# Router rows turned by DMA in an attention and mixture-of-experts kernel, with routing a half-step later

## The chip, the cores and the metric

The kernel runs on one core of a Trainium2 chip. The metric is the device time of one execution in microseconds, as the median over runs. The engines are named as in the profile: PE is TensorE (matmuls), with PEld its weight loads; DVE is VectorE, ACT is ScalarE, POOL is GpSimd, SP is SyncE, which issues most DMAs.

## What is computed

Gated cross-attention over a short context, then a mixture of experts, for 4 x 1024 tokens of width 256. Cut to what matters:

```python
x = x + tanh(g_xattn) * attn(layernorm(x), ctx, ctx, ...)     # 16 heads of 16, 77 keys, softmax(|q k| / 4)
n = layernorm(x)
logits = n @ w_router                                          # 256 x 8
probs = softmax(logits); topk_w, topk_idx = top_k(probs, 2)
h = gelu(n @ w1[e] + b1[e])                                    # 8 experts, 256 -> 1024 -> 256
out = sum over the two experts of topk_w[e] * (h @ w2[e] + b2[e])
x = x + tanh(g_ffn) * out
```

## The kernel before, in words

There are 32 tiles of 128 tokens; two tiles are a *pair*, 16 pairs in all. The attention phase goes through the pairs in half-steps: `even(j)` works on the scores of tile 2j, `odd(j)` on those of tile 2j + 1, and each half-step also carries a piece of work of older pairs. Every engine has its own `even` and `odd`, written out by hand, so the order on each engine is fixed in the program; semaphores (`ready`) order the engines against each other. The expert phase then takes tiles of 256 (later 128) routed rows.

What an older pair goes through in the kernel before, with j the pair of the half-step:

- `odd(j)`: the attention of pair j - 2 is projected into the bank PROJ (`project_attention`); VectorE adds it to x (`add_attention`, L1174) and takes the statistics of the sum (`row_statistics`).
- `even(j)`: GpSimd makes the factors (`norm_factors`), ScalarE the normalised rows of pair j - 3 (`normalise_row`) and their two-byte high half (`high_row`), which with the low half of `low_row` (VectorE, `odd(j)`) makes the row that is scattered to the experts.
- `odd(j)`: TensorE turns the normalised rows of pair j - 3 (`turn_rows`, four 128x128 transposes in four-byte values into the bank TURN), ScalarE copies them (`copy_rows`), TensorE multiplies them by the router's weights (`router_logits`, L1673) into the bank ROUTE, VectorE copies the logits out (`route(j, 1)`, L1142).
- `even(j)`: VectorE picks the two experts of pair j - 4 (`choose`), TensorE counts ranks (`ranks`, L1682 to L1686), VectorE makes the rows' places (`place_rows`) and the shares.
- `odd(j)`: GpSimd scatters the rows of pair j - 4 with four indirect DMAs (`scatter_rows`).

PROJ, TURN, NORM and ROUTE are the four banks that the scores use too. So TensorE waits ahead of each half-step's scores (`score_banks_free`) until what was left in them has been read; for the even half-step that is also `x2_sb`, the addition of the attention of the pair in the half-step before.

In the same half-steps the experts' weights are loaded and split: SyncE loads half a layer into `stage`, ScalarE makes the two-byte high half (`high_half`), VectorE the low half (`low_half`, L1128), and SyncE loads the next half once the low half is done. VectorE also splits the projected queries (`low_queries`, L1347) behind ScalarE's `high_queries`, and finds the largest score per head (`top_scores`, L1091).

After ten pairs have been routed (`EARLY_PAIRS`), VectorE plans the first six expert tiles (`plan_early`), so that the experts can begin before the last pairs are routed.

## Time and profile before

| | |
|---|---|
| Median of 3 runs | 660.27 us (655.99 to 662.45) |
| The profiled execution | 654.93 us, its span 653.1 us |
| Busy share of the span | PE 97%, PEld 86%, DVE 70%, ACT 51%, POOL 48% |
| Granted TensorE clock, mean | 0.989 |
| Attention phase, up to the first expert tile | some 258 us of the span |

The rows further down come from views of this one execution. The stretches give, between two times, how long each engine was busy, the granted TensorE clock (PEclk, 1.00 is full speed) and the share of the DMA engines. The timeline gives an engine's instructions in order of time, equal ones in a row merged; a bracket at a row's end is the idle time before it and what ended it. Matmul ends are modelled, so starts are what to compare on PE. The page's part on DMA issues and the view of one line give the time from a DMA's issue to its landing.

### The profile page before, as it was taken

The numbers are of one execution on the slowest core, as the hardware profiler recorded it, in microseconds if no ns is written. First come the engines' busy times: TensorE is split into PE (matmuls) and PEld (weight loads), VectorE is DVE, ScalarE is ACT, GpSimd is POOL, SyncE is SP. The second block draws the span as 40 slices with busy tenths as digits, with TensorE's granted clock in tenths as the row PEclk, the third lists the DMA queues.
The fourth block names the chain that finished last, engine by engine and source line by source line (L and its number), as shares of the span: only waits on it lengthen the run. The fifth ranks groups of instructions, "written<-read, shape, count | busy, mean of one in ns | idle before, by whom it ended". The sixth has DMA issues, their size and how long they took to land.

```text
span 653.1 us, 20940 instructions
## 1 busy us (share of the span) xinstructions
PE 633.6 (97%) x6637; PEld 562.7 (86%) x6638; DVE 459.7 (70%) x1298; ACT 333.8 (51%) x741; POOL 310.7 (48%) x420
## 2 busy tenths in 40 slices
PE   8999999999999999899999999999999999999993
PEld 7799999999999999798888888888888888888872
DVE  5687888888888896689665656556564647777773
ACT  4668777788778875623242323323242324444441
POOL 6423477777777455766352323334242433333333
PEclk9899999999999999899999999999999999999997
DMA  6144354555544445524954333333433344533322
GB/s 208 41 135 156 115 159 153 164 164 177 165 149 132 147 156 172 117 55 81 202 74 60 50 49 49 51 51 58 60 46 56 43 58 54 56 54 52 52 35 25
DMA packets 89157, 63.37 MB, mean 97 GB/s; under 512 B 51489, under 2 KB 84775, under 8 KB 88935
## 3 DMA queue, kind: packets, MB, share of 16 engines
q1 hardware_dynamic: 75519, 43.95, 26.0%
q0 software_dynamic: 13440, 18.14, 16.5%
q8 instruction: 58, 0.95, 0.6%
q14 instruction: 36, 0.29, 0.2%
q10 hardware_dynamic: 104, 0.04, 0.0%
HBM read 28.08 MB, written 24.63 MB: 81 GB/s over the span
## 4 chain that ended last, share of the span: by engine, by line
PE 57%; DMA 3%; DVE 2%; issue 1%; POOLq 0%; ACT 0%; SPq 0%; DVEq 0%; ACTq 0%
PE banks L1720 20%; PE banks L1703 20%; PE banks L1738 7%; PE banks L1752 7%; DMA out_dram<-prob_t,meta 2%; PE banks L1632 1%; DMA x_t<-routed 1%; PE banks L1659 1%; PE banks L1673 0%; PE banks L1613 0%; PE banks L1640 0%; DVE prob L1291 0%; POOLq L681 0%; DVE v_area L1293 0%; DVE top L1091 0%
## 5 line engine op out<-in xcount | busy, mean ns | idle before, releaser
L977 ACT ACTIVATE stage<-banks,bias_t 128x256 f32<-128x256 f32 x200 | 83.8, 470 | 169.6 <-PE banks L1703 157.1
L1703 PE MATMUL banks<-x_t,w_hi 128*128 128x256 f16 x800 | 133.9, 274 | 1.4 <-DMA x_t<-routed 1.4
L1720 PE MATMUL banks<-w,prob 128*128 x800 | 132.4, 273 | 0.6 <-DVE v_area L1293 0.6
L856 POOL DMA_INDIRECT out_dram<-prob_t,meta x46 | 74.7, 1625 | 99.7 <-DVE prob_t L1283 82.6
L1703 PE MATMUL banks<-x_t,w_lo 128*128 128x256 f16 x400 | 109.7, 274 | 0.0
L1720 PE MATMUL banks<-w,v_area 128*128 x400 | 109.1, 273 | 0.0
L1703 PEld LDWEIGHTS banks<-x_t,w_hi 128*128 x800 | 78.5, 98 | 11.1 <-issue 1.5
L986 ACT ACTIVATE stage<-banks,bias_t 128x128 f32<-128x128 f32 x168 | 52.6, 363 | 66.8 <-PE banks L1738 66.5
L1720 PEld LDWEIGHTS banks<-w,prob 128*128 128x128 f16 x800 | 78.1, 98 | 9.8 <-issue 0.8
L819 POOL DMA_INDIRECT routed<-row,pos x64 | 71.2, 1113 | 27.9 <-issue 14.6
L1632 PEld LDWEIGHTS banks<-v_area,prob_t 128*128 128x128 f32 x640 | 73.9, 192 | 4.3 <-DVE attn L1110 0.7
L1632 PE MATMUL banks<-v_area,prob_t 128*128 128x34 f32 (+1 forms) x640 | 77.2, 277 | 0.3 <-DVE attn L1110 0.3
L1738 PEld LDWEIGHTS banks<-x_t,w_hi 128*128 x672 | 58.1, 98 | 19.9
L1738 PE MATMUL banks<-x_t,w_hi 128*128 128x128 f16 x672 | 72.9, 219 | 0.0
L1263 DVE TENSOR_TENSOR v_area<-stage,prob 128x512 f16<-128x512 f32 x100 | 69.4, 694 | 3.4
L1279 DVE SCALAR_TENSOR_TENSOR prob_t<-banks,arena 128x256 f32<-128x256 f32 x50 | 21.0, 420 | 70.0 <-PE banks L1720 68.5
L842 POOL DMA_INDIRECT out_dram<-prob_t,meta x21 | 32.9, 1566 | 70.0 <-DVE prob_t L1311 57.4
L1738 PE MATMUL banks<-x_t,w_lo 128*128 128x128 f16 x336 | 64.3, 219 | 0.0
L1752 PE MATMUL banks<-w,prob 128*128 x168 | 62.9, 379 | 0.3 <-DVE v_area L1293 0.3
L1091 DVE TENSOR_REDUCE top<-prob 128x16 f32<-128x1232 f32 x32 | 45.8, 1431 | 21.2 <-ACT prob L896 21.2
L1261 DVE CAST prob<-stage 128x512 f16<-128x512 f32 x100 | 44.2, 442 | 15.4 <-ACT stage L977 13.5
L1613 PE MATMUL banks<-ident,prob 128*128 128x128 f32 x320 | 52.3, 279 | 0.1
(254 smaller groups left out, 1254.9 us busy)
## 6 DMA issues: line engine op xcount, KB each, us to landing
stage<-in_L_ffn_w_dram SPq DMA_DIRECT2D x32, 512.0 KB, 4.1
x_in<-in_x_dram SPq DMA_DIRECT2D x16, 256.0 KB, 3.6
x_res<-in_x_dram SPq DMA_DIRECT2D x16, 256.0 KB, 4.0
out_dram<-x_res SPq DMA_DIRECT2D x16, 256.0 KB, 2.9
routed<-turned SPq DMA_DIRECT2D x9, 265.0 KB, 4.8
out_dram<-prob_t,meta POOLq DMA_INDIRECT x67, 3.8
routed<-row,pos POOLq DMA_INDIRECT x64, 2.9
arena<-in_L_ffn_b_dram SPq DMA_DIRECT2D x1, 1024.0 KB, 7.8
```

Source lines behind the costliest of these rows:

```text
L819: pool.indirect_dma_start(routed[:, :], bass.IndirectOffsetOnAxis(ap=pos[:, held, tile, choice:choice + 1], axis=0), row[:, held, tile], N ...
L856: pool.indirect_dma_start(out[:, :], bass.IndirectOffsetOnAxis(ap=meta_of(j, pj)[:, b, E:E + 1].bitcast(U32), axis=0), y[:, pj, b], None, ...
L977: ins = act.activation(hid[:, c], H[:, q, c % PER * SLOTS:(c % PER + 1) * SLOTS], ACT.Gelu_apprx_tanh, bias=k.bias_t[:, bass.ds(e * HC + c ...
L986: ins = act.activation(small_part(hid_flat, q)[:, c * P:(c + 1) * P], H[:, q, c * P:(c + 1) * P], ACT.Gelu_apprx_tanh, bias=k.bias_t[:, ba ...
L1091: dve.tensor_reduce(top_part(i, 0), prob[:, i % 2, 0:SCORES].rearrange("p (h k) -> p h k", k=KEYS), AX.X, ALU.max).then_inc(top_sb, 1)
L1263: dve.tensor_tensor(h_lo[:, pj, part], hid[:, part], h_hi[:, pj, part], ALU.subtract)\
L1613: pe.matmul(T[:, g, c * P:(c + 1) * P], prob[:, i % 2, (first + c) * P:(first + c + 1) * P], k.ident[:], is_transpose=True, start=(c == 0) ...
L1632: mm = pe.matmul(V[:, first * VW:(first + n) * VW], prob_t[:, c, :], k.v_rows[:, b, c, 0:n * VW], start=(c == 0), stop=(c == PCH - 1), ski ...
L1703: mm = pe.matmul(H[:, q, c % PER * SLOTS:(c % PER + 1) * SLOTS], w[:, bass.ds(e, 1), i, c * P:(c + 1) * P].rearrange("p a n -> p (a n)"), ...
L1720: mm = pe.matmul(Y[pj][:, b * D:(b + 1) * D], h[:, pj, c, b * P:(b + 1) * P], w[:, bass.ds(e, 1), c, :].rearrange("p a n -> p (a n)"), sta ...
L1738: mm = pe.matmul(H[:, q, c % PER * P:(c % PER + 1) * P], w[:, bass.ds(e, 1), i, c * P:(c + 1) * P].rearrange("p a n -> p (a n)"), x[:, i], ...
L1752: mm = pe.matmul(Y[p][:, 0:width], h[p][:, c * P:(c + 1) * P], k.w2[:, bass.ds(e, 1), c].rearrange("p a i n -> p (a i n)")[:, 0:width], st ...
```

## The change

For pairs 0 to 11 (`TURNED_PAIRS = PAIRS - 4`) the rows are no longer turned by TensorE. SyncE turns the two-byte halves of the row, which lie in SBUF for the scatter anyway, with two transposing DMAs per pair (`turn_rows` on SyncE, in `odd(j)` for pair j - 3). TensorE multiplies them by two-byte halves of the router's weights, made once, 12 matmuls per pair (high by high, high by low, low by high, two chunks, two tiles), and does it a half-step later, in `even(j)` for pair j - 4. Everything behind it moves on by a half-step: `choose` to the end of VectorE's `even(j)`, `ranks` to `odd(j)`, `place_rows` and `shares` to VectorE's `odd(j)`, `scatter_rows` to the end of GpSimd's `even` of the next pair, `plan_early` to the start of VectorE's `even(15)`. The last four pairs keep the old way, and pair 12's copy of the turned rows comes behind both high halves on ScalarE. In VectorE's `odd(j)` the attention is added ahead of `low_half(j, 0)`, not behind it. The two-byte identity is read out of the four-byte one with a stride instead of being a copy. The diff, cut to its core:

```diff
@@ SyncE
+                    if 0 <= j - 3 < TURNED_PAIRS:
+                        turn_rows(j - 3)
+                def turn_rows(j):
+                    ready(sp, row_hi, j)
+                    ready(sp, row_lo, j)
+                    ready(sp, logit_ps, j - 1)
+                    for tile in range(2):
+                        sp.dma_start_transpose(rows_t[:, :, tile * P:(tile + 1) * P],
+                                               row[:, j % ROWS_HELD, tile, 0:D].bitcast(F16)).then_inc(rows_ld, 16)
@@ GpSimd, end of even(j); its odd(j) is empty now
+                    if exists(j - 5):
+                        scatter_rows(j - 5)
@@ ScalarE, odd(j)
                     if j > 0 and token_tile(i - 1):
                         copy_top(i - 1)
-                    if exists(j - 3):
-                        copy_rows(j - 3)
                     if exists(j):
                         high_half(j, 1)
+                    if j - 3 == TURNED_PAIRS:
+                        copy_rows(j - 3)
                     if exists(j + 2):
                         copy_normalised(j + 2)
+                    if exists(j - 4):
+                        route_exp(j - 4)
@@ VectorE, even(j)
+                    if j - 5 == EARLY_PAIRS:
+                        plan_early()
...
+                    if exists(j - 4):
+                        route(j - 4, 1)
...
                         normalise_attn(i - 2)
-                    if routed_pair:
-                        route(j - 4, 11, 1)
-                        route(j - 4, 12, 2)
+                    if exists(j - 4):
+                        choose(j - 4)
@@ VectorE, odd(j)
                         normalise_attn(i - 2)
+                    if exists(j - 4):
+                        if j - 4 == EARLY_PAIRS:
+                            ready(dve, rank_ps, j - 4)
+                            count_early()
+                        place_rows(j - 4)
+                    if exists(j - 2):
+                        add_attention(j - 2)
+                        row_statistics(j - 2)
+                    if j - 3 == TURNED_PAIRS:
+                        route(j - 3, 1)
+                    if exists(j - 4):
+                        shares(j - 4)
                     if exists(j):
                         low_half(j, 0)
-                    if exists(j - 2):
-                        add_attention(j - 2)
-                    if exists(j - 3):
-                        route(j - 3, 1)
-                    if exists(j - 2):
-                        row_statistics(j - 2)
@@ TensorE
                 def router_logits(j):
-                    ready(pe, x2t_sb, j)
                     ready(pe, places, j - 1, PLACE_OPS, 1)
+                    if j < TURNED_PAIRS:
+                        ready(pe, router_halves, 0, 2)
+                        ready(pe, rows_ld, j, 32)
+                        for tile in range(2):
+                            n = 0
+                            for c in range(KC):
+                                for x, w in ((c, router_hi), (c, router_lo), (KC + c, router_hi)):
+                                    mm = pe.matmul(ROUTE[:, tile * E:(tile + 1) * E], rows_t[:, x, tile * P:(tile + 1) * P],
+                                                   w[:, c], start=(n == 0), stop=(n == 3 * KC - 1))
...
@@ TensorE, even(j): -ranks(j - 4)  +router_logits(j - 4)
@@ TensorE, odd(j)
-                    if exists(j - 3):
+                    if exists(j - 4):
+                        ranks(j - 4)
+                    if j - 3 == TURNED_PAIRS:
                         turn_rows(j - 3)
```

What stands where on TensorE, in the odd half-step of the full swing, between the turned largest scores (`top`) and the probabilities. Before:

```order
L1600 MATMUL banks<-ident_bf,top 128x128
L1640 MATMUL banks<-ident,turned 128x128 x4
L1659 MATMUL banks<-x_t,turned 128x256 x4
L1673 MATMUL banks<-w_router,turned 128x8 x4
L1640 MATMUL banks<-ident,x_norm 128x128 x4
```

The turn of the rows, the attention's projection (L1659), the router product, the turn of the new pair's x. In the changed kernel, at the same place:

```order
L1619 MATMUL banks<-ident,top 128x128
L1713 MATMUL banks<-chosen,before 128x8
L1714 MATMUL banks<-seen,ones 128x8
L1715 MATMUL banks<-chosen,before 128x8
L1716 MATMUL banks<-seen,ones 128x8
L1717 MATMUL banks<-chosen,ones 128x8
L1678 MATMUL banks<-x_t,turned 128x256 x4
L1659 MATMUL banks<-ident,x_norm 128x128 x4
```

The four turns and the four-byte product are gone, the five rank matmuls have come in. In the even half-step the ranks stood ahead of the projection of the queries (L1809) before; in the changed kernel the 12 router matmuls stand there, of which the last two and what follows them are:

```order
L1696 MATMUL banks<-router_lo,rows_t 128x8
L1696 MATMUL banks<-router_hi,rows_t 128x8
L1840 MATMUL banks<-xn_t,x_t 128x256 x4
L1659 MATMUL banks<-ident,attn 128x128 x4
L1632 MATMUL banks<-ident,prob 128x128 x4
```

So the projection of the queries is behind more matmuls than it was. On VectorE, in the odd half-step from the attention of the tile (`attn`) on, before:

```order
L1110 TENSOR_TENSOR attn<-banks,den 128x256
L1128 SCALAR_TENSOR_TENSOR w_lo<-stage,w_hi 128x1024
L1174 SCALAR_TENSOR_TENSOR x_res<-banks,gates,x_res 128x512
L1142 COPY logits<-banks 128x16
L1117 BN_STATS stats<-x_res 128x6 x2
L1123 BN_AGGR mv<-stats 128x2 x2
L1145 MAX best<-logits 128x8 x2
```

In the changed kernel, at the same place:

```order
L1124 TENSOR_TENSOR attn<-banks,den 128x256
L1203 TENSOR_TENSOR place<-banks,region_of 128x16
L1206 TENSOR_TENSOR seen<-seen,chosen 128x8
L1208 TENSOR_TENSOR placed<-mask,place 128x32
L1212 TENSOR_REDUCE pos<-placed 128x4
L1213 TENSOR_TENSOR seen<-seen,chosen 128x8
L1189 SCALAR_TENSOR_TENSOR x_res<-banks,gates,x_res 128x512
L1131 BN_STATS stats<-x_res 128x6 x2
L1137 BN_AGGR mv<-stats 128x2 x2
L1177 TENSOR_REDUCE l_sum<-l_exp 128x2
L1179 RECIPROCAL l_rec<-l_sum 128x2
L1182 TENSOR_TENSOR share<-l_exp,l_rec 128x4
```

The low half of the weights (`w_lo`) stands behind the shares now; the five instructions of `place_rows` have come in ahead of the addition of the attention (`x_res`).

## Rows read from the trace of the kernel before

**Rows 1.** Stretches: length, busy time by engine, PEclk, DMA share, GB/s.

```profile
core 0: us, PE busy (x) PEld busy (x) DVE busy (x) ACT busy (x) POOL busy (x), PEclk, DMA share, GB/s
70.82:220.78 149.96, 149.96 (x1713) 140.11 (x1712) 128.25 (x426) 117.83 (x221) 108.81 (x170) 1.00 0.49 158
220.78:248.89 28.11, 27.48 (x330) 25.69 (x328) 25.04 (x89) 21.59 (x41) 15.03 (x23) 1.00 0.56 158
```

**Rows 2.** Timeline of TensorE over one pair: start, length, instruction.

```profile
130.80 0.58 PE L1572 MATMUL banks<-arena 32*128 32x154 f16 x24
...
133.62 0.17 PE L1682 MATMUL banks<-chosen,before 128*128 128x8 bf16 x1
...
133.75 1.97 PE L1809 MATMUL banks<-xn_t,x_t 128*128 128x256 f32 x8
...
137.76 0.58 PE L1572 MATMUL banks<-arena 32*128 32x154 f16 x24
...
140.58 0.61 PE L1640 MATMUL banks<-ident,turned 128*128 128x128 f32 x4
141.03 1.89 PE L1659 MATMUL banks<-x_t,turned 128*128 128x256 f32 x8
142.76 0.95 PE L1673 MATMUL banks<-w_router,turned 128*128 128x8 f32 x8
143.57 0.63 PE L1640 MATMUL banks<-ident,x_norm 128*128 128x128 f32 x4
144.04 0.60 PE L1613 MATMUL banks<-ident,prob 128*128 128x128 f32 x4
```

**Rows 3.** Timeline of VectorE over the same pair.

```profile
136.64 0.88 DVE L1347 SCALAR_TENSOR_TENSOR arena<-banks,bias_t,arena 128x256 f16<-128x256 f32 x2 [0.23 <-ACT arena L912]
...
138.05 0.15 DVE L1164 RECIPROCAL l_rec<-l_sum 128x2 f32<-128x2 f32 x1
...
138.32 0.75 DVE L1117 BATCH_NORM_STATS2 stats<-x_in 128x6 f32<-128x256 f32 x2
...
139.33 0.66 DVE L1269 TENSOR_TENSOR row<-turned,row 128x512 f16<-128x512 f32 x1
...
142.08 1.22 DVE L1128 SCALAR_TENSOR_TENSOR w_lo<-stage,w_hi 128x1024 f16<-128x1024 f32 x1
143.22 0.74 DVE L1174 SCALAR_TENSOR_TENSOR x_res<-banks,gates,x_res 128x512 f32<-128x512 f32 x1
```

**Rows 4.** Timeline of VectorE: the choice of experts up to the placed rows.

```profile
236.36 0.20 DVE L1145 MAX8 best<-logits 128x8 f32<-128x8 f32 x2
...
237.61 1.43 DVE L1091 TENSOR_REDUCE top<-prob 128x16 f32<-128x1232 f32 x1
...
239.31 0.16 DVE L1188 TENSOR_TENSOR place<-banks,region_of 128x16 f32<-128x16 f32 x1
...
239.91 0.17 DVE L1097 TENSOR_TENSOR top<-top 128x16 f32<-128x16 f32 x1
```

**Rows 5.** One line, transposing DMAs of 256 rows from DRAM: length min/median/max, landing.

```profile
L1893 SPq DMA_TRANSPOSE x_t<-routed x25: 1237/1254/2882, 243.3 to 502.4; - x25
...
DMA to landing us min/median/max: 3.1/3.3/5.9
```

**Rows 6.** One line, transposing DMAs of 128 rows from DRAM.

```profile
L715 SPq DMA_TRANSPOSE x_t<-routed x21: 1204/1215/1240, 512.9 to 618.8; - x21
...
DMA to landing us min/median/max: 2.5/2.7/4.5
```

**Rows 7.** Timeline of VectorE: start of the early plan, and what follows it.

```profile
228.32 0.42 DVE L1222 TENSOR_TENSOR x_norm<-tile_no 128x256 f32<-128x256 f32 x1
...
230.66 0.68 DVE L1269 TENSOR_TENSOR row<-turned,row 128x512 f16<-128x512 f32 x1
```

**Rows 8.** The page's DMA issues: KB each, median us to landing.

```profile
stage<-in_L_ffn_w_dram SPq DMA_DIRECT2D x32, 512.0 KB, 4.1
```

**Rows 9.** Timeline of ScalarE in the last odd half-step.

```profile
244.85 0.60 ACT L971 ACTIVATE turned<-banks 128x512 f32<-128x512 f32 x1 [0.17 <-PE banks L1640]
246.32 1.06 ACT L935 ACTIVATE w<-stage 128x1024 f16<-128x1024 f32 x1 [0.87 <-DMA stage<-in_L_ffn_w_dram]
```

More of the change, by code:

```diff
@@ L72 @@
 LAST_PAIRS = PAIRS - 3
+TURNED_PAIRS = PAIRS - 4
 LATE_FULL = FULL_TILES - EARLY_TILES
@@ L526, in main_phase @@
         attn_t, x2_t = turned[:, 0], turned[:, 1]
+        rows_t = sb("rows_t", [P, 2 * KC, PAIR], F16)
+        router_hi, router_lo = (sb(n, [P, KC, E], F16) for n in ("router_hi", "router_lo"))
         pad_rows = turned[:].rearrange("p a c n -> p (a c n)")[:, 0:SB * ROW].rearrange("p (b r) -> p b r", b=SB)
@@ L940, in normalise_row @@
                     if j < LAST_PAIRS:
-                        ready(act, logit_ps, j - 1)
+                        ready(act, row_lo, j - 1)
                     elif j == LAST_PAIRS:
@@ L968, in copy_rows @@
                 def copy_rows(j):
-                    ready(act, x2t_ps, j)
+                    ready(act, x2t_ps, j - TURNED_PAIRS)
                     ready(act, row_lo, min(j, LAST_PAIRS - 1))
@@ L1141, in route @@
                     if part == 1:
-                        dve.tensor_copy(logits[:].rearrange("p t e -> p (t e)"), ROUTE[:, 0:2 * E]).then_inc(router, 1)
+                        dve.tensor_scalar(logits[:].rearrange("p t e -> p (t e)"), ROUTE[:, 0:2 * E],
+                                          1.0 / W_SCALE if j < TURNED_PAIRS else 1.0, None, ALU.mult).then_inc(router, 1)
                     if part == 2:
@@ L1352, in even @@
                     i = 2 * j
[L1353 to L1356 removed]
+                    if j - 5 == EARLY_PAIRS:
+                        plan_early()
+                    if exists(j):
                         top_scores(i)
                         split_top(i, 1)
[L1359 to L1364 removed]
+                    if exists(j - 4):
+                        route(j - 4, 1)
+                    if exists(j):
                         split_top(i, 2)
@@ L1403, in odd @@
                         normalise_attn(i - 2)
+                    if exists(j - 4):
[10 more added lines that the diff above has]
+                        shares(j - 4)
                     if exists(j):
                         low_half(j, 0)
-                    if exists(j - 2):
-                        add_attention(j - 2)
-                    if exists(j - 3):
-                        route(j - 3, 1)
-                    if exists(j - 2):
-                        row_statistics(j - 2)
+                dve.tensor_scalar(router_hi[:], k.w_router[:], W_SCALE, None, ALU.mult).then_inc(router_halves, 1)
+                dve.wait_ge(router_halves, 1)
+                dve.scalar_tensor_tensor(router_lo[:], k.w_router[:], W_SCALE, router_hi[:], ALU.mult, ALU.subtract)\
+                    .then_inc(router_halves, 1)
                 low_values()
                 pipeline(even, odd)
-                even(PAIRS)
+                choose(PAIRS - 4)
+                place_rows(PAIRS - 4)
+                low_half(PAIRS - 1, 1)
+                inverse_sums(TILES - 2)
+                normalise_attn(TILES - 2)
+                shares(PAIRS - 4)
                 add_attention(PAIRS - 2)
@@ L1554, in score_banks_free @@
                         ready(pe, ot_sb, min(j - 2, PAIRS - 1), KC)
+                        ready(pe, router, j - 4, ROUTER_OPS, 1)
+                    else:
+                        ready(pe, x2_sb, min(j - 2, PAIRS - 1))
+                        ready(pe, xt_sb, min(j + 2, PAIRS - 1))
                         ready(pe, places, j - 4, PLACE_OPS, 1)
@@ L1557, in score_banks_free @@
                             ready(pe, early_plan, 0)
-                    else:
-                        ready(pe, x2t_sb, j - 3)
-                        ready(pe, x2_sb, min(j - 2, PAIRS - 1))
-                        ready(pe, xt_sb, min(j + 2, PAIRS - 1))
-                        ready(pe, router, j - 3, ROUTER_OPS, 1)
                 def scores(i):
@@ L1650, in turn_attention @@
                     ready(pe, attn_sb, j, 2)
-                    ready(pe, x2t_sb, j - 2)
+                    ready(pe, x2t_sb, j - 2 - TURNED_PAIRS)
                     turn_pair(TURN, attn, ot_ps)
@@ L1668, in router_logits @@
                 def router_logits(j):
-                    ready(pe, x2t_sb, j)
                     ready(pe, places, j - 1, PLACE_OPS, 1)
+                    if j < TURNED_PAIRS:
[7 more added lines that the diff above has]
+                                                   w[:, c], start=(n == 0), stop=(n == 3 * KC - 1))
+                                    n += 1
+                        mm.then_inc(logit_ps, 1)
+                        return
+                    ready(pe, x2t_sb, j - TURNED_PAIRS)
                     for tile in range(2):
@@ L1803, in even @@
                     if exists(j - 4):
-                        ranks(j - 4)
+                        router_logits(j - 4)
                     if follows(j + 1):
```

32 lines of the change are left out of this document (6 added, 26 removed).

## Prediction

> **What bounds the kernel now.** I read the stretches first. In the 149.96 us from 70.82 to 220.78, ten pairs of token tiles in full swing, TensorE is busy for all 149.96 us at the full clock (PEclk 1.00, the 2.4 GHz level); VectorE is busy for 128.25 us of them, that is 12.8 us of each pair's 15.00 [rows 1]. So a pair costs what TensorE has to do for it, and nothing else shows. Then TensorE's timeline of one pair: the even half-step starts with its scores at 130.80, the odd one at 137.76, so even is 6.96 us and odd 8.04 us, without a wait between the starts [rows 2]. Behind this stand the last two pairs, 28.11 us with 27.48 us busy [rows 1], and then the experts, where TensorE is also the bound; no instruction of theirs is changed. The change therefore acts on sixteen pairs of attention, and on what their end looks like.
>
> **What it takes off and puts on TensorE.** For pairs 0 to 11 the odd half-step loses the four turns of the normalised rows (140.58 to 141.03, 0.45 us) and the four-byte router product (142.76 to 143.57, 0.81 us) [rows 2]. The ranks, five small matmuls with 8 moving columns, go from even to odd: 133.62 to 133.75, 0.13 us, or 0.026 us each [rows 2]. The even half-step gets 12 router matmuls on two-byte halves. The trace has none on these operands; from below their price is the ranks' 0.026 each (same 128x128 two-byte weights, same 8 columns), from above the old product's, 0.81 us for 8 records, 0.10 each [rows 2]. That is 0.32 to 1.2 us for twelve. I take 0.32, since weights and columns are those of the ranks. Even becomes 6.96 + 0.32 - 0.13 = 7.15 us, odd 8.04 - 0.45 - 0.81 + 0.13 = 6.91 us, a pair 14.06 us instead of 15.00: 0.94 us off, 11.3 us over twelve pairs, if nobody else becomes late. The identity read with a stride of two costs nothing in my sum: one matmul per tile in 32 tiles, whose moving side has the pitch of the four-byte turns beside it.
>
> **Who becomes late: VectorE.** The scores of the next even half-step overwrite the bank from which VectorE's addition of the attention reads, so TensorE waits there for that addition. In the new order it stands behind a chain that starts with the low halves of the queries, which wait for TensorE's projection. They started at 136.64, 5.84 us into the pair, and now start 0.19 later, at 6.03. From there: low queries, reciprocal and the even tile's attention to 138.05, 1.41 us (the sum over exponentials that stood between them goes, but the reciprocal has to end anyway); the choice of experts, now here, 236.36 to 237.61, 1.25 us; the statistics of x up to the odd tile's attention, 138.32 to 142.08, 3.76 us; placing the rows, 239.31 to 239.91, 0.60 us; the addition, 0.74 us [rows 3, 4]. That ends at 13.79 us. TensorE would come to the scores at 14.06, so there is 0.27 us for the hand-over and for slower instructions. Had the low half of the weights (142.08 to 143.22, 1.14 us [rows 3]) stayed ahead of the addition, it would end at 14.93 and take back nearly all of the gain; this is what the swap buys. The rest of VectorE's odd half-step then ends some 2.3 us into the next pair and its idle time ahead of the queries takes that up; 12.8 us of work fit into 14.1. I take 14.15 us for a pair, with 14.06 (no hand-over) and 14.25 as bounds: 0.85 us off (0.75 to 0.94).
>
> **Who else moves.** GpSimd's four scatters per pair start behind x's normalisation instead of behind a wait for the shares; its work per pair is unchanged, 108.81/10 = 10.9 us busy [rows 1]. The addition began 2.58 us ahead of the next pair (143.22 of 145.80, which is 130.80 + 15.00) and now begins 1.1 us ahead (13.05 of 14.15), so the row factors and ScalarE's normalisation behind it come 1.5 us later in the pair; ScalarE idles ahead of the projected queries, and I take it that this holds them. ScalarE loses one copy per pair. These cost nothing while the queries' copies on ScalarE are not late; if they were, each tenth goes into the pair.
>
> **The transposing DMAs.** SyncE issues two per pair, 128 rows of 512 two-byte values each, from SBUF, behind the wait for the rows' low halves. Low rows end 6.03 + 1.41 + 1.25 + 1.01 (138.32 to 139.33) + 0.66 = 10.36 us into the pair [rows 3, 4], and TensorE wants both at 14.15 + 2.82 (130.80 to 133.62) = 16.97: 6.6 us. The trace has transposing DMAs from DRAM only. For 128 rows: 1.22 us on SyncE, 2.7 us from issue to landing [rows 6]; for 256 rows 1.25 us and 3.3 us, at worst 2.88 us and 5.9 us [rows 5]. With the 128-row medians the second lands at 10.36 + 1.22 + 2.7 = 14.3; with the worst row for both, 10.36 + 2.88 + 5.9 = 19.1. I take the medians' row, same size; 2.7 us of cover are left. If the cover is gone, TensorE waits at the router product, and with it everything behind it. Queued behind the two on SyncE are the store of x2, the next x and the weights' first half; 2.4 us of issue end at 12.8, before the first of them is ready to go (13.79).
>
> **The end of the phase.** Before, these two pairs take 28.11 us [rows 1]. Even half-step 14: 7.15. Odd 14 has no turn of new rows (143.57 to 144.04, 0.47 [rows 2]): 6.91 - 0.47 = 6.44. There VectorE skips the statistics of x (1.01), so its addition ends at 12.8; with statistics of x2 (1.0, as of x), shares (0.4, an estimate from 138.05 to 138.32 for two of their three) and low half (1.14 [rows 3]) it is free at 15.4, which is 1.8 us into half-step 15 (13.6). Now the early plan comes, 228.32 to 230.66, 2.34 us [rows 7], which stood a half-step earlier; it ends at 4.15. The reduction and its split (237.61 to 239.31, 1.70 [rows 4]), a few small ones, the low half (1.14), reciprocal and attention (0.7) end at 7.8. TensorE wants this attention at about 6.0: it waits 1.8 us. It then runs on to the router product of pair 12, still in the old way, at about 12.4. But its copy now stands behind ScalarE's second high half, whose load SyncE can issue only when VectorE's low half is done at 7.1. The load takes 4.1 us in the median [rows 8], say up to 5.1; the high half 1.06, the copy 0.60 [rows 9]: 12.9 to 13.9. Another 0.5 to 1.5 us. With the product (0.81) and the probabilities (1.7) this half-step pair ends at 15.5 to 16.5, the three together at 29.1 to 30.1: 1.0 to 2.0 us longer than before.
>
> **The sum.** Odd half-step 3 loses 1.26 us (its ranks did not exist either way), ten pairs lose 8.5 us (7.5 to 9.4), the last two gain 1.5 us (1.0 to 2.0). That is 8.2 us off, bounds 6.8 to 9.7. Behind it the orders of TensorE are the same up to the wait for the second expert tile's rows, which starts from the last projection and so moves along. The profiled execution took 654.93 us and would take 646.7. The runs' median, 660.27, is 5.3 us above it; so I forecast 660.27 - 8.2 = 652.1, rounded to 652.0.
>
> **Rivals.**
>
> First, the turned rows land late (the other side). One mechanism: the wait of TensorE at the router product. With the slow rows above (2.88 and 5.9) the second lands at 19.1, 2.1 us late in each of twelve pairs: 12 x 2.1 = 25 us against 8.2 gained, about 677. It decides against the change from 8.2/12 = 0.7 us late on, so if the two take more than 7.3 us together. For it: slow ones exist, and a source in SBUF is not in the trace. Against: the medians of 25 and of 21 are 3.3 and 2.7 [rows 5, 6]. The Trainium skill ("VectorE: DVE Perf Modes", Rules for kernel authors and the three transpose paths) speaks against the change: a 128x128 turn belongs on TensorE if PSUM will do as its goal, 390 ns against 1309 ns by the DMA crossbar. Eight such blocks one after another would be 10.5 us, an estimate from that page, so late by 3.9 us. The trace does not agree that they add up: 256 rows are eight such blocks and landed in 3.3 us [rows 5]; and no run here shows one from SBUF. Chance of a loss over 1% by this: 0.14.
>
> Second, VectorE takes it back. If the chain to the addition is 0.3 to 0.5 us longer than my rows (it now runs beside GpSimd's normalisation and scatters at other moments), the pair is 14.4 to 14.6 and ten pairs give 4 to 6 us; less the end's 1.5 and plus 1.26, some 4 to 6 us in all: 655 to 656. The same result comes from the end, if the waits there let TensorE's clock fall. Or from turned rows that are late by a few tenths. Within 1%: 0.32.
>
> Third, the change does less than it says, because the twelve router matmuls cost 0.10 each: even grows by 1.07 instead of 0.19 and the pair is back at 14.94, so no measurable change, with the end's loss about 660. The ranks' rows speak against it: 0.04.
>
> **Chances and range.** My forecast 0.5; the first rival 0.14; the second 0.32; the third 0.04. 1% (6.6 us) is about what a measurement of this kernel can tell from no change. Faster 0.5, same 0.35, slower 0.15. The range goes from 645.5 (all bounds at their best, 9.7, and a run some 5 us under the median, as 655.99 is) to 662.0 (second and third rival); above lies the first.
>
> **What would show it.** Right: a pair of 14.1 to 14.3 us on TensorE; twelve router matmuls in about 0.3 us with no wait ahead; VectorE's addition ending a few tenths before the next scores; one wait of 1 to 2 us for the attention and one for the copied rows in the last pair. Wrong: waits at the router product that name the DMA; waits ahead of the even scores that name the addition; a span of the ten pairs near 150 us; a low clock behind the last pairs.

## The result, and the profile after

The changed kernel took 685.06 us (median, 683.57 to 686.31), the kernel before on the same chip 660.16 us: a ratio of 1.0384 [1.0326, 1.0441]. Forecast were 652.0 us and a range of 645.5 to 662.0. The change costs 25 us where 8 were to be gained.

The head of the page of the profile after: span, busy time by engine, and of the 40 slices TensorE's busy share and granted clock.

```profile
span 684.5 us, 20929 instructions
PE 648.2 (95%) x6637; PEld 569.1 (83%) x6638; DVE 467.3 (68%) x1300; ACT 326.1 (48%) x729; POOL 317.3 (46%) x419
PE   7899998999998988989999999999999999999993
PEclk9999997997997977899999999999999999999997
```

The granted clock has dents in six of the slices 7 to 17 (17.1 us each), the part with the attention and the start of the experts; behind them only the last slice has one. Stretches of the kernel after, in the columns of [rows 1]:

```profile
70.82:220.78 149.96, 141.23 (x1494) 127.25 (x1493) 117.59 (x381) 98.36 (x186) 94.66 (x143) 0.90 0.54 153
122.00:136.00 14.00, 14.00 (x173) 12.96 (x172) 12.54 (x43) 11.10 (x21) 10.55 (x16) 1.00 0.66 181
147.60:151.00 3.40, 2.42 (x39) 1.81 (x37) 2.60 (x9) 2.00 (x4) 2.27 (x4) 1.00 0.81 229
151.00:157.80 6.80, 6.80 (x37) 5.97 (x37) 3.00 (x5) 3.03 (x7) 5.62 (x12) 0.50 0.48 139
```

The first row is the stretch of [rows 1]: TensorE, which was busy for 149.96 us of it at the full clock, is now idle for 8.73 us and has a mean clock of 0.90. The second row is a stretch as it was meant: no idle time, full clock. The third and fourth show the disturbance: 0.98 us idle out of 3.40 at the full clock, and right behind it 6.80 us at 0.50, which is the 1.2 GHz level. In that time TensorE is busy throughout, at half the clock.

TensorE's timeline of the kernel after, first a pair that is undisturbed, then the beginning of the next:

```profile
126.68 0.58 PE L1591 MATMUL banks<-arena 32*128 32x154 f16 x24
...
133.64 0.58 PE L1591 MATMUL banks<-arena 32*128 32x154 f16 x24
...
136.41 0.23 PE L1619 MATMUL banks<-ident,top 128*128 128x128 bf16 x1
136.47 0.17 PE L1696 MATMUL banks<-router_hi,rows_t 128*128 128x8 f16 x1
...
136.75 0.17 PE L1696 MATMUL banks<-router_hi,rows_t 128*128 128x8 f16 x1
...
140.78 0.58 PE L1591 MATMUL banks<-arena 32*128 32x154 f16 x24
...
147.31 0.39 PE L1632 MATMUL banks<-ident,prob 128*128 128x128 f32 x2
147.54 0.28 PE L1637 MATMUL banks<-top_t,spread_top 128*128 128x128 bf16 x2
147.78 0.61 PE L1591 MATMUL banks<-arena 32*128 32x154 f16 x16
148.88 0.37 PE L1591 MATMUL banks<-arena 32*128 32x154 f16 x8 [0.49 <-issue]
149.74 3.31 PE L1651 MATMUL banks<-v_area,prob_t 128*128 128x34 f32 x20 [0.50 <-ACT prob_t L938]
```

From one odd half-step's scores to the next (126.68 to 140.78) are 14.10 us; odd is 6.96 and even 7.14. The 12 router matmuls start at 136.47 right behind the row ahead of them and take about 0.3 us. Then TensorE halts in the middle of its scores, for 0.49 us up to 148.88 and for no wait that the profile can name, and up to 149.74 it waits 0.50 us for ScalarE. The twelve pairs from 3 on take, by the starts of their odd scores, 13.94, 14.10, 18.74, 18.04, 14.10, 18.76, 17.91, 14.10, 18.73, 18.43, 16.73 and 18.40 us: 202.0 together, where the same twelve took 178.2 before (62.79 to 240.97 in its trace). So 24 of the 31 us between the two spans (684.5 and 653.1) are there. Most of the rest lies right behind: from 264 to 310 us TensorE's clock is 0.85 on the mean and it is idle for 5.3 us, where before, 21 us earlier, it was 0.96 and 2.6.

The totals of TensorE's waits from 70 to 250 us, by what ended them:

```profile
PE banks L1651 <- issue: 5.4, 12, 1.0
PE banks L1591 <- issue: 1.7, 3, 0.7
PE banks L1651 <- ACT prob_t L938: 1.5, 3, 0.5
```

No line names the router product or a DMA; before, all waits of this stretch together were 0.5 us. And the waits of "issue" are TensorE's own. What ScalarE sees in that moment stands in its timeline of the kernel after, and what GpSimd does in GpSimd's, the first two rows of the undisturbed pair and the last four of the disturbed one:

```profile
149.00 1.36 ACT L938 ACTIVATE prob_t<-banks 128x512 f32<-128x512 f32 x3 [2.12 <-PE banks L1637]
```

```profile
127.94 1.11 POOL L835 DMA_INDIRECT routed<-row,pos  x1 [0.82 <-POOL row L827]
...
132.36 0.96 POOL L835 DMA_INDIRECT routed<-row,pos  x1 [0.30 <-issue]
...
143.02 1.10 POOL L835 DMA_INDIRECT routed<-row,pos  x1 [0.82 <-POOL row L827]
144.42 0.97 POOL L835 DMA_INDIRECT routed<-row,pos  x1 [0.30 <-issue]
145.70 0.96 POOL L835 DMA_INDIRECT routed<-row,pos  x1 [0.31 <-issue]
146.96 0.96 POOL L835 DMA_INDIRECT routed<-row,pos  x1 [0.30 <-issue]
```

ScalarE starts on the turned probabilities at 149.00, though by the profile's row the last of them were at TensorE at 147.54 for 0.28 us. The trace's records of semaphore increments say what lies between: TensorE dispatches its instructions on time, but the increments that mark their completion come late, by up to 2.1 us for these turned probabilities, and by 3.0 to 3.8 us for scores at other places. ("Late" means beyond the shortest delay of the same line.) In one place the turn of x and the attention's projection are 1.7 and 2.1 us late as well. Some records are missing in this trace, but of the scores all are there. In the profile of the kernel before, which has all its records, none of the 300 increments between 70 and 250 us is late by more than 0.3 us. TensorE's dispatch runs ahead for a while and then halts, which the profile calls issue. Each such time lies in, or at the end of, the four scatters that GpSimd issues: here 143.02 to 147.92, 2.24 to 7.14 us into an odd half-step of 6.96 us, so that the last reaches into the next scores. In the undisturbed pair they run from 1.26 to 6.64 us and end ahead of the next scores; the turned probabilities, from 5.20 us on, lie under them there too, and are late by 0.5 us at most. In the kernel before, they ran from 2.09 to 7.63 in an odd half-step of 8.04 us. The last two, in GpSimd's timeline of the kernel before, stand beside the turned probabilities of [rows 2] (from 144.04 on), which were on time:

```profile
142.53 1.60 POOL L819 DMA_INDIRECT routed<-row,pos  x1 [0.30 <-issue]
144.44 0.96 POOL L819 DMA_INDIRECT routed<-row,pos  x1 [0.31 <-issue]
```

So it isn't enough that scatters and turned probabilities meet.

### The profile page after: what moved, and what is told of

It is laid out like the page before. It is cut to its first block, busy times and chain, and to the rows that moved or that the text cites. A ratio compares the mean times of both kernels' runs of the same rounds, so it can differ in the third digit from the quotient of the medians.

```text
span 684.5 us, 20929 instructions
## 1 busy us (share of the span) xinstructions
PE 648.2 (95%) x6637; PEld 569.1 (83%) x6638; DVE 467.3 (68%) x1300; ACT 326.1 (48%) x729; POOL 317.3 (46%) x419
## 4 chain that ended last, share of the span: by engine, by line
PE 49%; DVE 4%; DMA 3%; issue 2%; ACT 0%; POOLq 0%; DVEq 0%; SPq 0%; ACTq 0%
PE banks L1751 19%; PE banks L1734 19%; PE banks L1769 5%; PE banks L1783 5%; DMA out_dram<-prob_t,meta 2%; DVE prob L1306 1%; DMA x_t<-routed 1%; DVE v_area L1308 1%; PE banks L1678 1%; ACT stage L1000 0%; DVE prob_t L1323 0%; DVE prob_t L1319 0%; PE banks L1651 0%; PE banks L1659 0%; PE banks L1632 0%
## 5 line engine op out<-in xcount | busy, mean ns | idle before, releaser
L1651 PE MATMUL banks<-v_area,prob_t 128*128 128x34 f32 (+1 forms) x640 | 82.4, 283 | 8.1 <-issue 5.4
L1651 PEld LDWEIGHTS banks<-v_area,prob_t 128*128 128x128 f32 x640 | 78.3, 198 | 12.9 <-issue 8.0
L1734 PEld LDWEIGHTS banks<-x_t,w_hi 128*128 x800 | 78.7, 99 | 10.8 <-issue 1.2
L1751 PEld LDWEIGHTS banks<-w,prob 128*128 128x128 f16 x800 | 78.1, 98 | 10.5 <-issue 1.4
L835 POOL DMA_INDIRECT routed<-row,pos x64 | 65.8, 1028 | 27.9 <-issue 14.6
L938 ACT ACTIVATE prob_t<-banks 128x512 f32<-128x512 f32 (+1 forms) x96 | 45.9, 535 | 20.5 <-PE banks L1637 17.9
```

The lines of the kernel that those rows point to most:

```text
L835: pool.indirect_dma_start(routed[:, :], bass.IndirectOffsetOnAxis(ap=pos[:, held, tile, choice:choice + 1], axis=0), row[:, held, tile], N ...
L938: act.activation(prob_t[:, first:first + n, :].rearrange("p c n -> p (c n)"), T[:, g, 0:n * P], ACT.Exp, scale=DH ** -0.5).then_inc(pt_sb, 1)
L1651: mm = pe.matmul(V[:, first * VW:(first + n) * VW], prob_t[:, c, :], k.v_rows[:, b, c, 0:n * VW], start=(c == 0), stop=(c == PCH - 1), ski ...
L1734: mm = pe.matmul(H[:, q, c % PER * SLOTS:(c % PER + 1) * SLOTS], w[:, bass.ds(e, 1), i, c * P:(c + 1) * P].rearrange("p a n -> p (a n)"), ...
L1751: mm = pe.matmul(Y[pj][:, b * D:(b + 1) * D], h[:, pj, c, b * P:(b + 1) * P], w[:, bass.ds(e, 1), c, :].rearrange("p a n -> p (a n)"), sta ...
```

## The experiments

The theories, by the letters that stand in the expectations: **T**, the transposing DMAs hold up TensorE; **S**, it is the scatters' new place; **P**, the faster pace as such brings the loss; **V**, VectorE's swapped order (the addition ahead of the low half) does; **K**, a sharpening of S: scores and turned probabilities don't get on while GpSimd issues scatters, so it counts which work of TensorE they fall on; **L**, the load of scatters and transposes together, in any order. Ratios are to the kernel before on the same chip.

**The transposing DMAs alone.** The kernel before, with the two DMAs per pair added; nobody reads what they write. It also reads the two-byte identity with a stride, as the changed kernel does.

```diff
+                    if 0 <= j - 3 < PAIRS - 4:
+                        turn_rows(j - 3)
```

> The kernel before, with the change's two transposing DMAs per pair added on SyncE for pairs 0 to 11 (into a tile that nobody reads); TensorE still turns the rows itself. Theory T (the transposing DMAs out of SBUF hold TensorE up while they run): pairs of 18 to 19 us appear among the 15.0 us ones, clock falls in the ten pairs, 675 us or more. Theory S (GpSimd's scatters at their new place hold it up) and theory P (only a TensorE that runs a pair in 14.1 us runs into it): pairs stay at 15.0 us, 655 to 663 us.

667.14 us, 1.0128 [1.0003, 1.0253]. Pairs take 15.0 to 15.6 us, two of them 19.2 and 17.4. Turned probabilities complete about 1 us late, and they do so under the scatters. So these DMAs, with the identity's stride, cost some 8 us by themselves, not 25; with two runs the interval reaches from almost nothing to 2.5%, and the time lies between what T and what S and P had expected.

**No transposing DMAs.** The kernel after, but TensorE turns the rows and multiplies four-byte values as before; logits, routing and scatters stay a half-step later.

```diff
-                    if 0 <= j - 3 < TURNED_PAIRS:
-                        turn_rows(j - 3)
...
+                    if exists(j - 3) and j - 3 != TURNED_PAIRS:
+                        copy_rows(j - 3)
```

> The changed kernel without its transposing DMAs: TensorE turns the rows in the odd half-step and multiplies them by the router in four bytes, as before, but logits, routing and scatters stay the half-step later and VectorE's order stays the new one. TensorE's pair is then 15.0 us by its rows. Theory T: no stalls, ten pairs near 150 us, 655 to 664 us with the end of the phase 1 to 2 us longer. Theory S: stalls of 2 to 5 us remain, pairs of 18 us, over 675 us. Theory P: no stalls, 655 to 664 us.

716.54 us, 1.0878 [1.0791, 1.0965]: the loss without the DMAs is 58 us. T falls as the cause of the 25 us. The disturbed pairs take 20.4 to 21.2 us, most of them 20.4 to 20.5; in those the first scatter starts 0.11 to 0.13 us ahead of the odd scores, and these complete 2.9 to 3.7 us late. TensorE's largest group of waits from 70 to 250 us (total, times, longest):

```profile
PE banks L1716 <- issue: 17.6, 7, 2.6
```

The stretch itself, columns as in [rows 1]:

```profile
70.00:250.00 180.00, 159.52 (x1525) 143.55 (x1524) 118.34 (x382) 105.29 (x196) 94.33 (x146) 0.84 0.37 117
```

17.6 us in 7 waits ahead of the rank matmuls, and a clock of 0.84.

**The swap alone.** The kernel before, with the attention added (and its statistics taken) ahead of the low half.

```diff
-                    if exists(j):
-                        low_half(j, 0)
                     if exists(j - 2):
                         add_attention(j - 2)
...
+                    if exists(j):
+                        low_half(j, 0)
```

> The kernel before with VectorE's swap alone (attention and statistics ahead of the low half in the odd half-step). All theories: no stall, TensorE's 15.0 us a pair stay the bound, within 3 us of the kernel before (657 to 663 us).

667.88 us, 1.0146 [1.0095, 1.0196]: a miss, 657 to 663 was expected. Pairs take 15.1 to 15.8 us, two of them 16.9 and 17.2; turned probabilities are about 1.0 us late. A change that only lets VectorE be earlier costs 9 us here.

**Slower pace.** The kernel after, its router product issued four times over, which gives TensorE back the 0.9 us per pair.

```diff
-                        for tile in range(2):
+                        for again in range(4):
+                          for tile in range(2):
```

> The changed kernel with its twelve router matmuls issued four times over (the same result), 36 more of 0.026 us, so TensorE's pair is 15.0 us again while DMAs and scatters stay as changed. Theory T: the stalls stay, two pairs in three of 18 to 19 us, 685 us or more. Theory P: the stalls go, pairs of 15.0 us, 657 to 665 us. Theory S: stalls stay unless the shift of half a microsecond moves the scatters off the place, 665 to 690 us.

717.32 us, 1.089 [1.0801, 1.0978]. A TensorE with more work per pair loses more, so P falls. Most pairs take 20.2 to 21.4 us; the first scatter starts 0.13 to 1.8 us ahead of the odd scores in them.

**The kernel before, once more,** unchanged, to see what its own trace varies by.

> The kernel before, unchanged, once more on this chip with a profile. All theories: 656 to 662 us, pairs of 15.0 us without stalls. It shows whether the semaphore records that are missing in every changed kernel's trace while GpSimd issues its scatters are there when TensorE does not stall.

660.14 us, 0.999 [0.9946, 1.0034]. The time is as expected, the profile is not: in it (span 660.2, clock 0.983) pairs take 15.0 to 15.6 us, and turned probabilities under scatters are 0.4 to 1.3 us late. The kernel before has the stall too; the profile that the prediction was read from, 653.1 us, is one without it. Of 8238 semaphore records in the first trace of this kernel, this one has 7002, so its lateness is read with care. All traces but the first lack some; the records go missing with and without the change.

**The swap undone.** The kernel after, with the low half ahead of the addition again.

```diff
+                    if exists(j):
+                        low_half(j, 0)
                     if exists(j - 2):
                         add_attention(j - 2)
...
-                    if exists(j):
-                        low_half(j, 0)
```

> The changed kernel with the swap undone: the low half is again ahead of the attention in VectorE's odd half-step. Theory S (it is the new place of GpSimd's scatters against TensorE's work): stalls stay, two pairs in three of 18 us or more, 680 us or more. Theory V (the swap sets the stalls off, as it cost 9 us alone): the stalls go; TensorE then waits 0.8 us a pair for the attention, pairs of 14.9 to 15.0 us, 657 to 663 us.

698.18 us, 1.053 [1.0408, 1.0653]. V falls. The first pairs take 15.04 to 15.08 us, since TensorE waits for the addition, as the prediction had it for this order (the swap "buys" 0.9 us); then the stalls set in and pairs take 18 to 20.7.

**The scatters alone.** The kernel before; the only edit moves the scatters to where the kernel after has them, the end of GpSimd's even half-step of the next pair.

```diff
@@ GpSimd, end of even(j)
+                    if exists(j - 5):
+                        scatter_rows(j - 5)
@@ GpSimd, odd(j)
-                    if exists(j - 4):
-                        scatter_rows(j - 4)
```

> The kernel before with one thing changed: GpSimd issues the scatters of a pair behind the normalisation of x in the next even half-step, as the changed kernel does, instead of at the odd half-step's start. Theory S: pairs of over 15.5 us with stalls while the scatters are issued, 670 us or more. Theory V: pairs stay at 15.0 us, 657 to 663 us.

711.12 us, 1.0726 [1.0616, 1.0835]; pairs of 19.3 to 21.6 us. One disturbed odd half-step in the timeline of all engines of this kernel:

```profile
152.15 1.10 POOL L821 DMA_INDIRECT routed<-row,pos  x1 [0.82 <-POOL row L813]
...
152.20 0.58 PE L1572 MATMUL banks<-arena 32*128 32x154 f16 x24
...
154.97 0.22 PE L1600 MATMUL banks<-ident_bf,top 128*128 128x128 bf16 x1
155.84 1.20 ACT L896 ACTIVATE prob<-banks 128x1232 f32<-128x1232 f32 x1 [2.71 <-remote]
156.09 0.96 POOL L821 DMA_INDIRECT routed<-row,pos  x1 [0.30 <-issue]
...
157.09 0.47 PE L1640 MATMUL banks<-ident,turned 128*128 128x128 f32 x1 [1.90 <-ACT prob L896]
```

And the stretch behind it, columns as in [rows 1]:

```profile
156.00:166.00 10.00, 8.91 (x37) 8.07 (x38) 6.31 (x22) 4.84 (x7) 2.31 (x6) 0.50 0.24 77
```

The scores are at TensorE at 152.20 and should be done within a microsecond. ScalarE, which reads them, starts at 155.84 after 2.71 us of waiting; the profile finds no releaser ("remote"), and the semaphore records have the scores' completion at 155.71, 2.93 us late. The first scatter started at 152.15. TensorE waits for ScalarE from 155.19 to 157.09, and the clock is then 0.50 for 10 us. S stands: this one edit makes the loss, on the kernel before, with no DMA added and no pace changed.

**The same, held back by the scores.** The experiment above, with one wait ahead of the first scatter, for the odd scores of the same half-step.

```diff
+                    if exists(j + 5):
+                        ready(pool, score_ps, 2 * j + 11, 4)
```

> The kernel before with the scatters in the later place (the one that cost 51 us alone), but the first is issued only once the odd half-step's scores are done, 0.8 us later than there. Theory K: the 2.9 us ahead of the scores go, pairs of 15.0 to 15.5 us, 657 to 667 us. Theory L: stalls stay at whatever TensorE does then, 690 us or more.

658.55 us, 0.9977 [0.9939, 1.0015]. The whole loss of 51 us is gone. The same place in the program, in the timeline of all engines of this kernel:

```profile
154.54 0.58 PE L1574 MATMUL banks<-arena 32*128 32x154 f16 x24
...
155.31 1.24 ACT L898 ACTIVATE prob<-banks 128x1232 f32<-128x1232 f32 x1
...
156.19 1.55 POOL L823 DMA_INDIRECT routed<-row,pos  x1 [2.15 <-PE banks L1574]
...
157.37 0.61 PE L1642 MATMUL banks<-ident,turned 128*128 128x128 f32 x4
...
161.22 0.96 POOL L823 DMA_INDIRECT routed<-row,pos  x1 [0.30 <-issue]
```

And the same stretch:

```profile
156.00:166.00 10.00, 10.00 (x111) 9.50 (x111) 8.31 (x27) 7.96 (x14) 8.49 (x12) 1.00 0.61 205
```

GpSimd waits 2.15 us, the first scatter starts 1.65 us behind the scores, ScalarE reads them 0.77 us after they started (3.64 above), TensorE goes on without a wait and the clock stays at 1.00. Later by 1.7 us in the pair, the scatters cost nothing that the time shows. So it is their place against the scores that makes the loss, as K has it, and L's 690 us or more is out. But the last two scatters lie on the turned probabilities here as well, as in the kernel before; this pair of runs tells of the scores alone.

**Between scores and scores.** The kernel after, with the rows weighed earlier and the scatters behind the same wait for the odd scores, all four in the odd half-step.

```diff
-                        scatter_rows(j - 5)
+                        if exists(j):
+                            ready(pool, score_ps, 2 * j + 1, 4)
+                        send_rows(j - 5)
```

> The changed kernel with GpSimd's scatters moved by a microsecond only: the three small operations that weigh the rows stand ahead of x's normalisation, and the first scatter is issued behind it as soon as the odd half-step's scores are done, so that the four lie between some 0.8 and 6.2 us into the odd half-step, past the scores and mostly ahead of the turns of the probabilities (5.3 to 7.0). Theory K (TensorE's scores and turned probabilities do not get on while GpSimd issues scatters; elsewhere it does not matter): stalls of at most 0.5 us, pairs of 14.1 to 14.6 us, no clock falls in the ten pairs, 650 to 661 us. Theory L (it is the load of scatters, transposes and the rest in any order in a 14 us pair): stalls and falls of the clock stay, 675 us or more.

676.22 us, 1.0224 [1.0131, 1.0316]; K's 650 to 661 missed. The scatters now run from 1.5 to 6.4 or 6.7 us in the odd half-step and keep clear of the scores, which complete on time; but most of what TensorE does behind them is late: the ranks by 0.5 to 1.2 us, the projection and the turn of x by up to 2.4, the turned probabilities by up to 1.8. Pairs take 15.2 to 18.4 us. The turn of x of one pair at TensorE, and ScalarE's read of it in its own timeline:

```profile
112.61 0.60 PE L1668 MATMUL banks<-ident,x_norm 128*128 128x128 f32 x4
115.65 0.60 ACT L953 ACTIVATE xn_t<-banks 128x512 f32<-128x512 f32 x1 [3.56 <-remote]
```

To keep clear of the scores gives back 9 of the 25 us. That elsewhere the scatters' place doesn't matter, as K's expectation has it, is not borne out.

**Two by two.** The kernel after, with two scatters in the even half-step, behind the row factors, and two in the odd one, behind x's normalisation and the odd scores; shares go ahead of the row statistics on VectorE, so that the rows can be weighed at the start of the even half-step.

```diff
+                    if exists(j - 5):
+                        send_rows(j - 5, 0, 1)
...
-                        scatter_rows(j - 5)
+                        if exists(j):
+                            ready(pool, score_ps, 2 * j + 1, 4)
+                        send_rows(j - 5, 1, 2)
@@ VectorE, odd(j)
+                    if exists(j - 4):
+                        shares(j - 4)
                     if exists(j - 2):
...
-                    if exists(j - 4):
-                        shares(j - 4)
```

> The changed kernel with the four scatters of a pair split: the rows are weighed at the even half-step's start (VectorE's shares stand ahead of the statistics for that), two scatters are issued behind the row factors, some 3 us into the even half-step, two behind x's normalisation and past the odd scores, some 3 us into the odd one. Both places lie under TensorE's projections (2.9 to 5.3 us into a half-step). Theory K (scores and turned probabilities are what scatters hold up): pairs of 14.1 to 14.5 us without falls of the clock, 650 to 657 us, faster than both kernels. Theory L (transposes, scatters and the rest together are too much for a 14 us pair wherever they stand): stalls and falls of the clock as in the changed kernel, 675 us or more. Between them, 658 to 670 us, scatters under the projections cost too, but less.

661.23 us, 1.0047 [1.0027, 1.0068]. The kernel before took 658.76 us on this chip, so of the 25 us some 22 are gone, by the scatters' place and split (and the order of shares and statistics); all that the change did to TensorE and the DMAs is still there. Pairs take 14.1 to 16.3 us. The timeline of all engines over one odd half-step, with the last scatter ahead of it:

```profile
166.67 0.97 POOL L845 DMA_INDIRECT routed<-row,pos  x1 [0.30 <-issue]
...
167.40 0.58 PE L1604 MATMUL banks<-arena 32*128 32x154 f16 x24 [0.18 <-DVE arena L1374]
...
172.10 1.07 POOL L845 DMA_INDIRECT routed<-row,pos  x1 [0.18 <-issue]
...
172.67 0.60 PE L1645 MATMUL banks<-ident,prob 128*128 128x128 f32 x4
...
173.47 0.97 POOL L845 DMA_INDIRECT routed<-row,pos  x1 [0.30 <-issue]
```

The scatters come later than expected: not under the projections, but, at the full clock, 4.7 to 7.0 us into the odd half-step, on the turned probabilities, and the two ahead of it end 0.24 us behind the start of the odd scores. The turned probabilities are up to 1.0 us late. So this run doesn't test K's places; two scatters at a time, on the work that K names, cost little where four in a row cost 25 us. The stretch of 70 to 250 us, columns as in [rows 1]:

```profile
70.00:250.00 180.00, 172.01 (x1997) 157.55 (x1993) 157.96 (x509) 130.44 (x247) 127.73 (x187) 0.96 0.58 169
```

TensorE's two largest groups of waits in it:

```profile
PE banks L1604 <- issue: 3.3, 6, 0.6
PE banks L1664 <- DVE attn L1136: 2.8, 1, 2.8
```

What is left over is small stalls of the same kind (3.3 us at the scores, a clock of 0.96) and one wait for the attention. K's 650 to 657 were not reached, so the version that beats both kernels was not found.

**What stays open.** That GpSimd's four scatters, placed on the odd scores, hold up TensorE's completions is shown by the scatters' move alone and the wait that takes it back. For other work of TensorE it is seen (the turned probabilities, the ranks, the turn of x and the projection complete late under scatters or right behind them) but not separated: the turned probabilities are on time under scatters in the first profile of the kernel before. Whether the split or the place helped in the last run is not separated either; four scatters in a row were never set against two and two at the same place. By what path they act is not shown: whether the issue on GpSimd does it or the bytes that follow (that would need scatters of shorter rows, which were not run), and why dispatch goes on meanwhile. Nor is it shown why the transposing DMAs alone and the swap alone bring stalls of about 1 us under scatters that haven't moved in the program; L would have the load add up, but the run without the transposing DMAs, with less load and a larger loss, speaks against it as the main cause, while the last run would fit a load that counts by the half-step. And the same program before had no late completion in one profile and some in another.

## Why the prediction was wrong

**What bounded the kernel** was read rightly: TensorE in the attention, nothing else showing [rows 1, 2]. But a pair costs TensorE's work only at a full clock and with prompt completions, and both were taken as given.

**TensorE's work** came out as summed. The twelve router matmuls take 0.31 us (0.32 taken), even is 7.14 (7.15), odd 6.96 (6.91). The third rival, 0.10 for each, is out. A pair that nothing disturbs takes 14.10 us, inside the 14.06 to 14.25 given, 0.05 under the value taken. But only four of twelve are so, one of them at 13.94.

**VectorE's chain** was right to a tenth. Low rows and addition in the undisturbed pair of the timeline of VectorE after, whose even scores start at 119.55:

```profile
129.29 0.66 DVE L1284 TENSOR_TENSOR row<-turned,row 128x512 f16<-128x512 f32 x1
...
132.65 0.74 DVE L1189 SCALAR_TENSOR_TENSOR x_res<-banks,gates,x_res 128x512 f32<-128x512 f32 x1
```

Low rows end 10.40 us into the pair (10.36 forecast), the addition 13.84 (13.79), 0.25 us ahead of the next scores (0.27). That the swap buys most of this is borne out by the run that undoes it, whose first pairs take 15.04 to 15.08. The second rival, VectorE taking it back, didn't come about.

**The transposing DMAs** were in time. The pair that SyncE issues from 111.80 on, 2.51 us for the two, is wanted by TensorE at about 122.4; their data are there by 115.6 in the trace. That pair is a disturbed one; in the undisturbed pair shown above they are issued at 130.01, the last record of a landing is at 135.37, and the router product starts at 136.47, so 1.1 us of cover were left where 2.7 had been taken. No wait names them, so the first rival was not the way in which the change lost, though its sign was right. The Trainium skill ("VectorE: DVE Perf Modes", The three transpose paths) gives 1309 ns for a 128x128 turn by the DMA crossbar, as quoted ahead of the result, which if added up would be 10.5 us for the eight, an estimate; the trace doesn't agree that they add up for a source in SBUF either: 3.8 and 5.4 us from the first issue to the last landing in these two pairs. What they did cost, some 8 us when alone (with the identity's stride), was outside both readings: not late data but late completions on another engine.

**The step that failed is "Who else moves".** It saw the scatters move, "behind x's normalisation instead of behind a wait for the shares; its work per pair is unchanged", and costed the move at nothing as long as ScalarE's copies weren't late. It counted GpSimd's busy time and its order, and not what TensorE does in the moment when the scatters are issued. The wait for the shares, which the change replaced, had held the scatters at 2.09 us in the odd half-step, behind the scores, and an odd half-step of 8.04 us held them up to 7.63. The change shortened that half-step to 6.96 us, and put in place of that wait one that ends earlier. Sized by the runs: the move alone costs 51 us on the kernel before (711.12 against 660.16), and issuing them two by two gives back some 22 of the 25 us in the kernel after (661.23, against 658.76 before on that chip).

There is a rule that would have supported the failed step. The Trainium skill ("SBUF — State Buffer", Who interferes with whom) has it that a DMA doesn't contend with a compute engine and that "PE and ACT never wait on anyone". In this case scores complete 2.93 us late under four indirect scatters of GpSimd, and on time with the same four 1.65 us behind them; the measurement decides. Whether it is a port of that memory that they contend for, no run here shows.

**The size of the loss** comes from two parts, and the second is larger. From 70 to 250 us TensorE is idle for 10.8 us (169.19 of 180 busy, 0.6 before), and its clock is 0.91 on the mean, which is 16 us of full clock. A stall of 1 to 3 us is followed by 3.4 or 6.8 us at half the clock, 1.7 or 3.4 us of work. The prediction had named the clock only for the end of the phase.

**The end of the phase** can't be judged by its sum (1.0 to 2.0 us): it lies in stretches with a clock of 0.85. Of its two waits the one for the attention came, 1.8 us forecast, 1.2 in the kernel after and 2.8 in the run two by two; none names the copied rows in either.

## What to carry to other kernels

When an edit moves indirect scatters or other DMAs that GpSimd issues, look up which instructions of TensorE they will run beside, as one would for an engine's busy time; a wait ahead of them, or a split, may be worth more than the time it costs its own engine. A bound engine at 100% and full clock has no slack for a stall, and here it paid each twice, once for the idle time and once at half the clock behind it. Where a row of TensorE ends well before its reader starts and the profile says "issue" or "remote", the completion may be late, and the cause is worth seeking on another engine.

## What the runs showed of the hardware

- TensorE's instructions can be dispatched on time and complete 2.9 us late (3.0 to 3.8 for scores in the kernel after) while GpSimd issues four indirect scatters of 128 rows; with the first of the four 1.65 us behind their start, the scores are on time. The Trainium skill ("Perfetto Trace Analysis", Tensor Engine Instruction (MATMUL, LD_WEIGHTS)) states that TensorE's end time in a profile is an estimate; the trace agrees: the stalled scores have an end of 152.78 in their row, 2.9 us ahead of the increment.
- The clock fell behind such a stall, not in it: 1.00 from 147.60 to 151.00, where TensorE was idle for 0.98 us, and 0.50 from 151.00 to 157.80, where it was busy throughout.
- Pairs settle into a rhythm. Without the transposing DMAs the first scatter starts 0.11 to 0.13 us ahead of the odd scores in seven pairs one after another, and each takes 20.4 to 20.5 us. With the scatters moved alone, starts of 0.05 to 0.07 and of 2.5 to 2.8 us ahead take turns, with pairs of 19.3 to 21.6 us. In the kernel after, starts of 1.26 us behind the odd scores, 2.24 behind and some 2 us ahead take turns, a round of 51 us with one pair of 14.10 in it.
